# A windowed-attention, Mamba and mixture-of-experts layer on one core: masked keys, a product for the maxima, and the slots of two stages

## What is computed

```
# windows of 8x8 positions, 8 heads of 8 channels
qkv = xw @ qkv_w.T + qkv_b;  q, k = rope2(q), rope2(k)
h = softmax(q * 8**-0.5 @ k.T) @ v;  h = h @ proj_w.T + proj_b
# Mamba on g = layernorm(h): 128 inner channels, 16 states
xn = g * rsqrt(mean(g*g) + eps) * norm_w;  x, z = split(xn @ in_proj_w.T)
x = silu(causal_conv4(x) + conv_b);  delta = softplus(x @ projDelta_w.T + b)
state = exp(delta * A) * state + x * delta * B;  y = state . C + x * D
h = h + (y * silu(z)) @ out_proj_w.T + g
# six experts, three layers of 64 channels each; the router takes two
f = layernorm(h)
h = h + sum over the two best experts of weight * expert(f)
```

## Time and profile before

| | us |
|---|---|
| three runs: median (lowest, highest) | 1718.97 (1713.84, 1726.07) |
| the profiled execution, its own time | 1718.97 |
| its span, first to last instruction | 1717.1 |
| busy: TensorE / VectorE / ScalarE / GpSimd | 1282.1 / 1252.2 / 993.6 / 1090.7 |
| first scan starts at | 182.6 |
| last scan starts at | 1650.6 |

### The profile page before, as it was taken

One profiled execution on the slowest core, in us unless ns is written; L12 is line 12 of the kernel. 1 busy time (PEld: TensorE's weight loads), 2 busy tenths in 40 slices (PEclk: granted clock), 3 DMA queues, 4 the chain that ended last, 5 costly groups with the idle time before them and its releaser, 6 DMA issues. The chain is left out here.

```text
span 1717.1 us, 27116 instructions
## 1 busy us (share of the span) xinstructions
PE 1282.1 (75%) x8676; PEld 599.7 (35%) x8676; DVE 1252.2 (73%) x1451; ACT 993.6 (58%) x1861; POOL 1090.7 (64%) x1475
## 2 busy tenths in 40 slices
PE   2765867797877868797878878697978878775665
PEld 1442514253442525252433425252533424231221
DVE  1112578786978787887979777887968787989851
ACT  2224646657574756657575757667575757574422
POOL 2013577766767686766767676767767676977640
PEclk9966879888998989998998989998998989878775
DMA  2003679675858777776858677776758586878830
GB/s 71 3 15 81 159 194 228 178 204 155 246 160 227 198 205 193 194 204 162 238 155 227 180 209 203 204 199 176 224 154 234 159 227 197 244 214 254 223 74 6
DMA packets 215204, 303.82 MB, mean 177 GB/s; under 512 B 79436, under 2 KB 79640, under 8 KB 214936
## 3 DMA queue, kind: packets, MB, share of 16 engines
q1 hardware_dynamic: 215064, 302.10, 64.8%
HBM read 274.75 MB, written 20.97 MB: 172 GB/s over the span
## 5 line engine op out<-in xcount | busy, mean ns | idle before, releaser
L1282 POOL TENSOR_TENSOR hc<-hs,c_rep 128x512 f32<-128x512 f32 x512 | 651.3, 1274 | 334.2 <-DVE hs L1062 333.7
L1062 DVE TENSOR_TENSOR_SCAN hs<-bank,state,xd 128x512 f32<-128x512 f32 x512 | 643.6, 1271 | 67.5 <-issue 59.4
L802 ACT ACTIVATE bank<-dl,a_neg 128x512 f32<-128x512 f32 x512 | 351.8, 688 | 270.4 <-DVE hs L1062 261.9
L1052 DVE TENSOR_TENSOR xd<-xd,bank 128x1024 f32<-128x1024 f32 x256 | 306.5, 1197 | 48.3 <-DMA xd<-xdel_rows 41.5
L563 PE MATMUL bank<-q_diag,k_heads 128*128 128x128 f32 x1024 | 187.3, 308 | 5.0 <-ACT top_row L790 3.2
L563 PEld LDWEIGHTS bank<-q_diag,k_heads 128*128 128x128 f32 x1024 | 163.1, 197 | 57.9 <-issue 44.6
L456 PE MATMUL bank<-hc,wts 128*32 128x512 f32 x1024 | 162.8, 693 | 8.0 <-POOL hc L1282 4.2
L551 PE MATMUL bank<-k_heads,q_diag 64*64 64x512 f32 x512 | 89.7, 775 | 97.7 <-DMA q_diag<-rot 54.9
L621 PE MATMUL bank<-xz,wts 128*128 128x512 f32 x128 | 96.2, 843 | 79.3 <-ACT xz L902 70.0
L1082 DVE TENSOR_REDUCE neg_max<-bank 128x8 f32<-128x512 f32 x128 | 86.0, 677 | 83.5 <-PE bank L551 83.3
L446 PE MATMUL bank<-top_sel,zeros 128*128 128x512 bf16 x464 | 144.4, 417 | 0.0
(11 more groups left out here) (167 smaller groups left out, 2141.2 us busy)
## 6 DMA issues: line engine op xcount, KB each, us to landing
xd<-xdel_rows SPq DMA_DIRECT2D x512, 256.0 KB, 4.5
dl<-delta_rows SPq DMA_DIRECT2D x512, 256.0 KB, 4.2
delta_rows<-delta SPq DMA_DIRECT2D x16, 512.0 KB, 5.3
xdel_rows<-xdel SPq DMA_DIRECT2D x16, 512.0 KB, 3.4
xin<-in_x_dram SPq DMA_DIRECT2D x32, 128.0 KB, 2.6
q_diag<-rot SPq DMA_DIRECT2D x64, 64.0 KB
out_dram<-res SPq DMA_DIRECT2D x256, 16.0 KB
k_heads<-rot SPq DMA_DIRECT2D x128, 16.0 KB
```

The source lines that it names most:

```text
L802: act.activation(decay_bank(n)[:, :], dl[:, n % 4, :], ACT.Exp, scale=a_neg[:, g:g + 1])\
L1052: dve.tensor_tensor(pair, pair, b_ps[:, :].unsqueeze(1).to_broadcast([128, 2, BAND]), ALU.mult)\
L1062: dve.tensor_tensor_scan(hs[:, n % 4, :], decay_bank(n)[:, :], xd[:, n % 8, :], state[:, g:g + 1], ALU.mult, ALU.add).then_inc(scanned.sem, 1)
L1282: pool.tensor_tensor(hc[:, n % 8, :], hs[:, n % 4, :], c_rep[:, BAND * h:BAND * h + BAND], ALU.mult)\
```

## The change

- All eight masked heads of the keys are made by ScalarE, two at each of s = 5 to 8; the eight DMAs of `heads` on SP are gone.
- `top_row` becomes four rows of 128 columns, one for each head pair, masked by channel (four small ACTIVATEs instead of one), `top_sel` shrinks to two columns for each window, and the turned scores start with one bf16 product of 512 columns, on which the four fp32 products accumulate.
- Attention starts one slot earlier (slot 8), and all its steps from the scores on get s one higher, so they stay in their slots; the products before them, the rotation, the values and the queries' DMAs (slot 14) come one slot earlier, and the quotients stay in slot 8.
- Preparation moves: turning to slots 3 and 4, convolution 5 and 6, z 7, silu from slot 7 to 9, delta's products from 9 and 10 to 11 and 12, exp and ln from 11 to 13, the sums to slots 15 to 22, the stores to 21 and 23. Decay 10 is no longer early.
- The fillers are placed anew: 32 in a round.

```diff
-AT = {"S": [9, 11, 13, 15], "max": [9 + _w for _w in range(NW)],
-      "T": [18, 19, 21, 22, 24, 25, 27, 28], "P": [20, 20, 23, 23, 26, 26, 29, 29]}
-FILLERS = {10: 1, 11: 3, 13: 2, 14: 4, 16: 2, 17: 1, 23: 6, 24: 2, 25: 3, 26: 3, 29: 2}
-SOFT = (12, 15, 16, 17, 18, 19, 20, 21)
-EARLY = 10
+AT = {"S": [10, 12, 14, 16], "max": [10 + _w for _w in range(NW)],
+      "T": [19, 20, 22, 23, 25, 26, 28, 29], "P": [21, 21, 24, 24, 27, 27, 30, 30]}
+FILLERS = {10: 2, 12: 2, 13: 3, 14: 3, 15: 1, 16: 2, 17: 2, 22: 3, 23: 5, 24: 2, 25: 3, 26: 3, 29: 1}
+SOFT = (15, 16, 17, 18, 19, 20, 21, 22)
...
-            return (c + 3, n - 9) if n >= 9 else (c + 2, n + 23)
+            return (c + 3, n - 8) if n >= 8 else (c + 2, n + 24)
...
-                        if 13 <= n < 15:
-                            heads(c + 3, 4 * (n - 13), 4 * (n - 12))
-                        if n == 15:
+                        if n == 14:
                             queries(c + 3)
...
                     pe.wait_ge(A["top"].drained, A["top"].empty(k))
+                pe.matmul(use.bank[:, :], top_sel[:, 2 * w:2 * w + 2, :], top_row[:, :, :], start=True, stop=True)
                 for hp in range(4):
-                    at = slice(128 * hp, 128 * hp + 128)
-                    pe.matmul(use.bank[:, at], k_heads[:, w, 2 * hp:2 * hp + 2, :], q_diag[:, w, :], start=True, stop=True)
-                    row = HEADS * w + 2 * hp
-                    last = pe.matmul(use.bank[:, at], top_sel[:, row:row + 2, :], top_row[:, :],
+                    last = pe.matmul(use.bank[:, 128 * hp:128 * hp + 128], k_heads[:, w, 2 * hp:2 * hp + 2, :], q_diag[:, w, :],
                                      start=False, stop=True, skip_group_check=True)
...
-                if n == EARLY:
-                    if has(k + 2):
-                        act.wait_ge(A["P6"].drained, A["P6"].empty(k + 2))
-                elif n == EARLY + 2:
-                    act.wait_ge(scanned.sem, scanned.at(k, n - 3))
-                elif n > 1 or past(k - 1):
+                if n > 1 or past(k - 1):
                     act.wait_ge(scanned.sem, scanned.at(k, n - 1))
...
-                    copy(top_row[0:64, :], use.bank[0:64, 0:128]).then_inc(use.drained, 1)
+                    for hp in range(4):
+                        last = act.activation(top_row[0:64, hp, :], use.bank[0:64, 0:128], ACT.Copy, scale=top_mask[0:64, hp:hp + 1])
+                    last.then_inc(use.drained, 1)
...
-                if n == 7:
+                if n == 9:
                     tables("silu_and_others")
...
-                if n == 11:
+                if n == 13:
                     act.wait_ge(Bk["d1"].drained, Bk["d1"].empty(k))
...
-                if s in (5, 6):
+                if 5 <= s < 9:
                     for h in (2 * s - 10, 2 * s - 9):
```

More of the change, by code:

```diff
@@ L174, in tower @@
         neg_max = sb("neg_max", [128, NW, HEADS])
-        top_row = sb("top_row", [128, 128], BF16)
-        top_sel = sb("top_sel", [128, NW * HEADS, 64], BF16)
+        top_row = sb("top_row", [128, 4, 128], BF16)
+        top_sel = sb("top_sel", [128, NW * 2, 64], BF16)
+        top_mask = sb("top_mask", [128, 4])
+        top_few = sb("top_few", [128, NW * 2])
         zeros = sb("zeros", [128, 128], BF16)
@@ L241, in tower @@
         top_ready = sig("top_ready", 1)
-        heads_in = sig("heads_in", 12 * 16)
-        heads_act = sig("heads_act", HEADS // 2)
+        heads_in = sig("heads_in", 4 * 16)
+        heads_act = sig("heads_act", HEADS)
         rec_ready = sig("rec_ready", 1)
@@ L335, in spread_xdel @@
                 sp.dma_start(xd[:, n % 8, :], rows_of(xdel_dram, k, group(n), n // NU)).then_inc(xd_in[n % 8].sem, 16)
[L337 to L347, removed]
             def queries(k):
@@ L488, in attend_first @@
                     scores(k, 2 * AT["S"].index(s))
-                if s == 17:
+                if s == 18:
                     use = A["top"]
@@ L583, in prepare @@
             def prepare(k, q, n):
-                for s, i2 in ((2, 0), (3, 1)):
+                for s, i2 in ((3, 0), (4, 1)):
                     if n == s:
@@ L593, in prepare @@
                     at = BAND * h
-                    if n == 4 + h:
+                    if n == 5 + h:
                         use = Bk[f"conv{h}"]
@@ L778, in _ @@
             pe.wait_ge(placed, 192)
-            pe.wait_ge(setup_dve, 11)
+            pe.wait_ge(setup_dve, 13)
             pe.wait_ge(setup_pool, 15)
@@ L904, in prepare @@
                 for h in range(2):
-                    if n == 9 + h:
+                    if n == 11 + h:
                         use = Bk[f"d{h}"]
@@ L1007, in body @@
                     far = ahead(c, n, 2)
-                    if far and far[1] != EARLY:
+                    if far:
                         decay(*far)
@@ L1011, in body @@
                         values_out(k, s)
-                    if has(c) and n == EARLY - 3:
-                        decay(c, EARLY)
                     if has(c):
@@ L1038, in _ @@
             act.wait_ge(setup_pool, 15)
-            act.wait_ge(setup_dve, 11)
+            act.wait_ge(setup_dve, 13)
+            copy(top_sel[:, :, :], top_few[:, :].unsqueeze(2).to_broadcast([128, 2 * NW, 64])).then_inc(setup_act, 1)
             rounds(body)
@@ L1097, in attend, with reciprocals @@
                             op0=ALU.add, op1=ALU.mult).then_inc(use.drained, 1)
-                if s == 31:
+            def reciprocals(k, n):
+                if n == 8:
                     dve.wait_ge(A["P7"].drained, A["P7"].empty(k))
@@ L1221, in body @@
                     if has(c + 2):
+                        reciprocals(c + 2, n)
                         normalize(c + 2, n)
@@ L1242, in _ @@
                .then_inc(setup_dve, 1)
+            heads = col("ident", 0, 64).rearrange("p (w h b) -> p w h b", w=NW, h=4)
+            dve.tensor_reduce(top_few[:, :].rearrange("p (w b) -> p w b", w=NW), heads.rearrange("p w h b -> p w b h"), X_AXIS, ALU.add)\
+               .then_inc(setup_dve, 1)
+            dve.tensor_reduce(top_mask[:, :], heads.rearrange("p w h b -> p h w b"), mybir.AxisListType.XY, ALU.add)\
+               .then_inc(setup_dve, 1)
             dve.wait_ge(setup_pe, 1)
             dve.tensor_copy(h_bias[:, :], b_ps[:, 0:C]).then_inc(setup_dve, 1)
-            dve.wait_ge(setup_dve, 11)
+            dve.wait_ge(setup_dve, 13)
             dve.wait_ge(setup_pool, 15)
@@ L1298, in attend, with divide @@
                         pool.tensor_tensor(rot[:, i, :], rot[:, i, :], rot[:, 2 + i, :], ALU.add).then_inc(roped.sem, 1)
-                if s == 31:
+            def divide(k, n):
+                if n == 8:
                     pool.wait_ge(rec_ready.sem, rec_ready.at(k, 1))
@@ L1405, in body @@
                     if has(c + 2):
+                        divide(c + 2, n)
                         normalize(c + 2, n)
@@ L1424, in _ @@
             pool.wait_ge(setup_pool, 15)
-            pool.wait_ge(setup_dve, 11)
+            pool.wait_ge(setup_dve, 13)
             rounds(body)
```

33 lines of the change are left out of this document (14 added, 19 removed).

## The result

The changed kernel takes 1667.52 us (1659.62 to 1668.11), the kernel before in the same comparison 1721.49; the ratio is 0.968 (0.963 to 0.973). The forecast was 1666. The sum is right and its terms are not: of the 50.8 us between the two profiled spans (1717.1 and 1666.3), 16.4 lie before the first scan, where I had put 2, and the rounds gave less than forecast. The traces give TensorE's granted clock as 0.50 or as 1.00, and a stretch that holds both as their mean. A product is called cold at 0.50 and warm at 1.00: of two rows of the same size in the changed kernel, 64x512 fp32, h2_0's takes 1.98 us (0.50 from 855.3 to 857.3) and the first scores' 1.09 (1.00 from 861.4 to 864).

The account below looks back on a forecast made before the run. Waits bound the kernel: VectorE runs the scan and idles 17.7 of 95.4 us a round. Gains of 2.7 + 0.7 + 0.2 = 3.6 a round give 47, plus 4 and 2: 53 from 1718.97, so 1666 us, range 1626 to 1710.

Parts of the forecast that it names:

- The start, 2 us: The 183 us before the first scan would gain perhaps 2 us.
- Place A: Slots 5 to 8: shorter turned windows and preparation moved later bring scan 9 earlier, 2.7 us a round, bounds 1 and 4.
- one convolution of 1.8 leaves, and with another 0.23: TensorE's work ahead of scan 8's decay shrinks by these, so scan 8 comes 2.9 us earlier.
- Place B: Slots 9 to 12: work no longer waits behind silu and its table loads on ScalarE; gain 1.8 us a round.
- Slots 12 to 16, relu at 24.5: Denser ScalarE work after silu loses 1.1 us; experts' relu 24.5 us after scan 9 (25.2 before), bounds 22 and 29.
- the exp wait: Slot 15: VectorE would newly wait 2.1 us for the softplus' exp.
- Place C: Slots 16 to 18: the 2.5 us xdel wait goes, but VectorE waits 3.6 for the first scores; gain 0.2 a round.
- of which 0.64 was waiting for the queries: Relu to scores: 8.3 us before, 0.64 of it waiting for the queries, so 8.1 after the change.
- h1_1 in the cold state: TensorE product between relu and scores, taken to run at half speed still, read at 1.97 us.
- Sum over like rounds: One round's 3.6 us gain, times thirteen rounds with all stages, gives 47 us.
- stays warm: Rival: TensorE stays warm between h1_0 and h2_0 or warms sooner, 2.6 us more a round; 1632 us, chance 0.17.
- The merged product saves nothing: Rival: each window keeps 1.36 us, scan 8 comes 0.9 later, gain 2.3 a round; 1685 us, chance 0.08.

Follow-up runs that it names:

- keys_alone: Kernel before with all eight masked heads by ScalarE at slots 14 to 17 and without the eight masked-key DMAs; 1662.8 us, ratio 0.966.
- small_products: Changed kernel with four bf16 products of 128 columns again in each window, all else as changed; 1661.1 us, 0.966 of the kernel before.
- prep_alone: Kernel before with only preparation, silu, delta's products, exp and ln, sums and stores in later slots, and no early decay 10; 1626.0 us, ratio 0.945.
- softplus_12: Changed kernel with ScalarE's exp and ln at the end of slot 12 instead of 13; 1625.6 us, 0.942 of the kernel before.
- all_three: Changed kernel without the earlier start of attention and with the fillers of before; 1614.7 us, 0.937 of the kernel before.
- warm_wait: Changed kernel with 16 fillers instead of 2 in slot 16; 1659.2 us, 0.964 of the kernel before.
- product_alone: Kernel before with the maxima brought by one bf16 product of 512 columns per window instead of four of 128; 1702.5 us, ratio 0.989.
- prep_keys: Kernel before with preparation in its later slots and all masked heads by ScalarE at slots 14 to 17, attention's slots as before; 1611.2 us, ratio 0.936.
- all_three_warm: Changed kernel without the earlier start of attention, with the fillers of before but 16 instead of 2 in slot 16; 1617.2 us, 0.940 of the kernel before.

## Why the prediction came out right

The number was right by luck, through two errors that cancel: 14 us too little for the start, 17 too much for the rounds. Even the 92.1 us of the five alike rounds, against 91.8 forecast, came about otherwise than forecast. Such a round is 1.6 ahead of the kernel before at scan 9 (2.7 forecast), 1.1 at the relu (3.4) and 2.0 at the first maxima (3.6). The other 1.2 of its 3.3 come after the maxima, where I had nothing: the clock does not fall in slots 25 to 27 of these rounds (1.00 from 881 to 889 in round 7), as it did in six of the eleven before (0.50 from 924.2 to 931.0 in round 7).

- *The start, 2 us.* Wrong: 16.4. The term had no working. Rows before the first scan would have given most of it: three times 3 to 4 us from rotation to maxima for the DMAs. keys_alone shows 10.7 for them. The remaining 5.7 came with the rest: with four small products again (small_products) 5.2 of them are lost.
- *Place A, 2.7 a round.* Measured 1.6. Its account holds where TensorE stays warm: prep_alone gets 2.6, without the merged product (granted clock 1.00 from 800 to 821 in its round 7). The step that failed is "one convolution of 1.8 leaves, and with another 0.23": it assumed a warm TensorE, and in the changed kernel the clock falls in slots 5 and 6 (0.50 from 816.2 to 819.5 in round 7). The window itself was right (1.13 forecast, 1.10 measured). "Busy without a break from 844 to 868" was not exact: the 0.47 of idle time before 854.37 lies in it.
- *Place B, 1.8.* Measured 1.5: scan 12 comes 9.9 after scan 9 against 9.7 forecast. Silu hides as said. At scan 15 the stretch from scan 9 has won even 3.2 (14.9 for 18.2).
- *Slots 12 to 16, relu at 24.5.* Measured 25.8 in the undisturbed rounds. The wait for the router's copy was 1.66 and not 0.95, and decay 16 and the relu stand behind everything. One slot takes back what was won: scan 16 comes 22.3 after scan 9, against 20.9 before. I had named the exp wait (2.1 forecast, 2.9 measured) but had taken it as a matter of sums. softplus_12 and all_three show that it is one of order.
- *Place C, 0.2, "what the DMAs cost is turned into a wait for TensorE".* The wait is there, but 2.9 and not 3.6, and keys_alone wins 3.2 a round, where I had said 0.6. Two steps failed, both read from one round: "of which 0.64 was waiting for the queries" (1.4 in the mean) and "h1_1 in the cold state" (1.23 us in the mean after the change, not 1.97). "903.35" stands in no row either: it carries 809.02 over to the next round, whose first scores start at 902.88, 7.9 after the relu and not 8.3. The relief is worth much alone and nothing in a steady round once preparation is moved.
- *Sum over like rounds.* I multiplied one round by thirteen. Three of the rounds 2 to 12 are 4 to 7 us longer, with the clock low in slots 13 and 14 and again in 25 to 27 (in round 8 0.50 from 932.1 to 935.5 and from 973.2 to 983.3); one round is no sample.

Of the rivals, "stays warm" had the right chain (relu to maxima 1.5 shorter in warm_wait) and the wrong worth: not 34 us but 8 at most. "The merged product saves nothing" is refuted for the window, which falls from 1.36 to 1.10 us, and for the kernel before, where product_alone is at 0.989. Within the changed kernel the merged product is worth 5 us at the start and nothing in the whole, and the clock falls in another place with it than without it.

The rows of the kernel before spoke against the rival of the merged product. The 1.36 of a window are 0.34 us for each pair of an fp32 and a bf16 product, where the fp32 product alone takes 0.22, so the four bf16 ones cost 0.48 a window and a merged one 0.25; that saves 0.23, an estimate from these rows, and the rows after show 0.26. The rival's 0.9 for scan 8 stands in no row of the kernel before; product_alone has scan 9 0.9 earlier. That busy time ahead of h2_0 would keep it warm was not shown by a row of the kernel before either. warm_wait has it warm, with 16 fillers ahead of it (h2_0 1.09 us after 1.55 of idle time, at 1.00, and in the changed kernel 1.98 after 4.57, at 0.50), and that is no clear gain in the time of the kernel.

prep_keys, at 0.936 of the kernel before, beats both kernels; all_three and all_three_warm lie within 6 us of it.

## What to carry to other kernels

Try the parts of a change alone and in pairs: here they win 60, 20 and 97 us alone, 54 together with an earlier start and new fillers, and 108 without those. Where an engine takes its pieces in a written order, ask for every moved piece what now stands ahead of the one that another engine waits for; two ACTIVATEs in the wrong slot cost 42 us. Before a time is taken from one round, look at the same place in ten: the clock and a DMA's wait differed from round to round here (clock 0.98 and 0.66 over slots 24 to 27 in rounds 7 and 8 of the changed kernel; 0.64 and 1.40 us of waiting for the queries in rounds 6 and 7 of the kernel before). And price the start and the end by their own rows: nothing covered there what the steady rounds had been expected to hide (the keys' DMAs, 10.7 us at the start in keys_alone).

## What the runs showed that I had not expected

Making TensorE faster or warmer at one place went with a low clock at another (0.50 in slots 5 and 6 with the merged product and the new fillers, from 816.2 to 819.5 in round 7, and in slots 24 to 27 in warm_wait, from 877.9 to 881.3), which took back most of the gain or more. Kernels with different work settle on the same round: 88.7 us in prep_alone and prep_keys and 88.7 to 88.8 in seven rounds of softplus_12, 92.2 in keys_alone and 92.0 to 92.3 in five rounds of the changed kernel. In prep_keys all of them are within 0.2 us, with the clock falling at the same two places (from slots 17 and 22 on) each time, in round 7 to 0.50 from 826.2 to 833.0 and from 846.7 to 850.1. That rounds keep step with the clock is my reading of these rows; what holds a round at its value was not tried, and stays open.
